# A causal mask moved from two bf16 products a row block into the VectorE row maximum

## The reference

```
phi    = tp @ W_combine.T                      # 512 x 64 features of a sequence
logits = einsum('bnd,bmd->bnm', phi, phi) * T / temp
logits = where(n >= m, logits, -inf)           # causal
attn   = softmax(logits)
out    = (attn @ V) @ W_out.T + b_out
```

## Time and profile before

| | before |
|---|---|
| median of 3 runs | 726.18 us (725.48 to 726.43) |
| span of the profiled execution, first to last instruction | 729.0 us |
| PE busy | 707.8 us (97%) |
| PE weight load busy | 558.7 us (77%) |
| DVE busy | 620.3 us (85%) |
| ACT busy, POOL busy | 424.9 us (58%), 387.0 us (53%) |
| mean granted TensorE clock | 0.992 of full speed |

### The profile page before, as it was taken

How to read it: one execution, slowest core, us unless ns; L and a number is a source line. 1 busy time by engine, 2 the same in 40 slices (tenths; PEclk the granted TensorE clock), 3 DMA queues, 4 the chain that set the end, 5 groups by cost and what they waited for, 6 DMA issues and landing times.

```text
span 729.0 us, 15002 instructions
## 1 busy us (share of the span) xinstructions
PE 707.8 (97%) x4592; PEld 558.7 (77%) x4592; DVE 620.3 (85%) x1899; ACT 424.9 (58%) x840; POOL 387.0 (53%) x828
## 2 busy tenths in 40 slices
PE   7998999999999999999999999999999999999896
PEld 4977777777797887778697787879788777867684
DVE  5887888788989898998989899898989899887865
ACT  4539475736456584656648574655757565565441
POOL 4526577363565646476564747556574646653300
PEclk9889999999999999999999999999999999999999
DMA  7341111112423050323214042322304132121004
GB/s 217 112 145 43 45 28 32 29 31 65 111 89 87 6 155 16 116 59 117 58 47 129 3 125 51 116 58 79 98 1 144 31 117 59 59 59 59 1 7 167
DMA packets 49110, 54.12 MB, mean 74 GB/s; under 512 B 6214, under 2 KB 40584, under 8 KB 49032
## 3 DMA queue, kind: packets, MB, share of 16 engines
q1 hardware_dynamic: 48258, 52.64, 25.7%
q10 hardware_dynamic: 774, 0.53, 0.3%
HBM read 20.65 MB, written 16.78 MB: 51 GB/s over the span
## 4 chain that ended last, share of the span: by engine, by line
PE 85%; DVE 5%; DMA 2%; ACT 2%; POOL 2%; issue 2%; SPq 0%; DVEq 0%; ACTq 0%; POOLq 0%
PE ps L438 17%; PE ps L317 16%; PE ps L343 15%; PE ps L466 6%; PE ps L409 6%; PE ps L515 5%; PE ps L500 4%; PE ps L579 4%; PE ps L388 4%; PE ps L559 2%; PE ps L478 2%; POOL Z L254 2%; PE ps L390 2%; DMA xmT<-Z 1%; DMA X<-in_x 1%
## 5 line engine op out<-in xcount | busy, mean ns | idle before, releaser
L438 PE MATMUL ps<-VS,ET 128*128 128x257 f32 x640 | 159.4, 383 | 0.8 <-ACT ET L769 0.5
L438 PEld LDWEIGHTS ps<-VS,ET 128*128 128x128 f32 x640 | 112.5, 189 | 24.3 <-issue 11.7
L254 POOL TENSOR_TENSOR Z<-Z,QB 128x512 f32<-128x512 f32 x60 | 76.5, 1275 | 98.0 <-ACT Z L750 96.3
L708 ACT ACTIVATE xn<-X,rs 128x256 f32<-128x256 f32 x128 | 66.3, 592 | 73.3 <-POOL rs L1322 73.2
L769 ACT ACTIVATE ET<-ps 128x128 f32<-128x128 f32 (+3 forms) x128 | 55.2, 436 | 69.3 <-PE ps L317 67.9
L343 PE MATMUL ps<-W1h,xh 128*128 128x354 f32 x256 | 88.9, 347 | 0.2 <-DVE xl L889 0.2
L902 DVE TENSOR_TENSOR VS<-ps,biasM 128x354 f32<-128x354 f32 x128 | 66.3, 522 | 24.8 <-PE ps L343 24.7
L759 ACT ACTIVATE E<-ps,nmax 128x128 f32<-128x128 f32 (+3 forms) x128 | 64.3, 525 | 35.7 <-DVE nmax L971 34.2
L343 PE MATMUL ps<-W1l,xh 128*128 128x354 f32 x256 | 84.2, 329 | 0.0
L343 PE MATMUL ps<-W1h,xl 128*128 128x354 f32 x256 | 83.3, 325 | 0.0
L264 POOL TENSOR_SCALAR xm<-X,rs 128x256 f32<-128x256 f32 x120 | 65.8, 562 | 4.7 <-POOL rs L1343 4.7
(11 more groups left out here) (210 smaller groups left out, 1678.9 us busy)
## 6 DMA issues: line engine op xcount, KB each, us to landing
X<-in_x SPq DMA_DIRECT2D x32, 512.0 KB, 4.3
xmT<-Z SPq DMA_DIRECT2D x120, 128.0 KB, 2.3
out_x<-X SPq DMA_DIRECT2D x30, 512.0 KB, 3.9
out_x<-X SPq DMA_DIRECT2D x4, 256.0 KB, 2.2
X<-in_gru_whhT SPq DMA_DIRECT2D x1, 768.0 KB
wih<-in_gru_wihT SPq DMA_DIRECT2D x1, 768.0 KB
X<-in_W_v ACTq DMA_DIRECT2D x1, 256.0 KB, 4.3
X<-in_W_outT ACTq DMA_DIRECT2D x1, 256.0 KB, 5.0
```

The costliest lines, as they stand in the source:

```text
L254: e.tensor_tensor(Z[:, i + 1, :], Z[:, i, :], QB[:, :], ALU.mult).then_inc(s["zm"], 1)
L438: ins = e.matmul(p[:, 0:D + 1], ET[:, r % 2, j * 128:j * 128 + 128], VS[:, (2 * k + d) % 4, j, 0:D + 1], start=j == 0, stop=j == i)
L708: ins = e.activation(xn[:, d, t, :], X[:, b % NX, t, :], ACT.Identity, bias=rs[:, d, 2, t:t + 1], scale=rs[:, d, 1, t:t + 1])
```

## The change

The two mask products of each row block and their constants `identb` and `maskb` go. In their place stands one SBUF tensor `causal` of 128 x 512 fp32: zero, and +1e30 above the diagonal in its last 128 columns. `U` gets the opposite sign, so that the logits in PSUM are negated. `row_max` is now an operation that adds the last w columns of `causal` to the w negated logits, writes the sum back over them in PSUM, and keeps the minimum of each row; this minimum is the `nmax` of before. `expo` reads with scale -1. The program lists of all engines are written out in other words (loop bounds as numbers, breaks elsewhere), and `warm` now holds the wait that stood ahead of it.

```diff
-        identb = sb("identb", [128, 3, 128], BF)
-        maskb = sb("maskb", [128, 3, 128], BF)
+        causal = sb("causal", [128, N])
...
                     for d in range(2):
                         at["lg", 8 * k + 2 * i + d] = banks[d][:, c:c + w]
                         e.matmul(banks[d][:, c:c + w], QK[own(d), 0, rows], QK[own(d), 1, 0:w], start=True,
-                                 stop=False, skip_group_check=True)
-                    for d in range(2):
-                        e.matmul(banks[d][:, c + w - 128:c + w], identb[own(d), 1 - d, :], maskb[own(d), 1 - d, :], start=False,
-                                 stop=False, skip_group_check=True)
-                    for d in range(2):
-                        e.matmul(banks[d][:, c + w - 128:c + w], identb[own(d), 2 - d, :], maskb[own(d), 2 - d, :], start=False,
                                  stop=True, skip_group_check=True).then_inc(s["lg_mm"], 1)
...
-                e.activation(E[:, r % 3, 0:w], at["lg", r], ACT.Exp,
-                             bias=nmax[:, r % 8:r % 8 + 1]).then_inc(s["E"], 1)
+                e.activation(E[:, r % 3, 0:w], at["lg", r], ACT.Exp, bias=nmax[:, r % 8:r % 8 + 1],
+                             scale=-1.0).then_inc(s["E"], 1)
...
-                e.tensor_reduce(nmax[:, r % 8:r % 8 + 1], at["lg", r], AX.X, ALU.max,
-                                negate=True).then_inc(s["nmax"], 1)
+                w = (n // 2 + 1) * 128
+                e.tensor_tensor_reduce(at["lg", r], at["lg", r], causal[:, N - w:N], 1.0, 3e38, ALU.add, ALU.min,
+                                       nmax[:, r % 8:r % 8 + 1]).then_inc(s["nmax"], 1)
...
-                e.tensor_scalar(U[:, :], U[:, :], tmp8[:, 8:9], None, ALU.mult).then_inc(s["soft"], 1)
+                e.tensor_scalar(U[:, :], U[:, :], tmp8[:, 8:9], -1.0, ALU.mult, ALU.mult).then_inc(s["soft"], 1)
...
-            e.affine_select(out=maskb[:, :, :], in_=maskb[:, :, :], compare_op=ALU.is_ge, fill=-1e30,
-                            base=-64, pattern=[[64, 3], [-1, 128]], channel_multiplier=1).then_inc(s["const_chain"], 1)
+            e.affine_select(out=causal[:, N - 128:N], in_=causal[:, N - 128:N], compare_op=ALU.is_ge, fill=1e30,
+                            base=0, pattern=[[-1, 128]], channel_multiplier=1).then_inc(s["const_chain"], 1)
```

More of the change, by code:

```diff
@@ L651, in _ @@
[L651 to L659, removed]
-                p, n, f, m, g = it + 2, it + 1, it, it - 1, it - 2
[L661 to L681, removed]
+            first_warm(); weights_setup(); xn_t(0, 0, 0); xn_t(0, 0, 1); bias_setup(); xn_t(0, 1, 0)
@@ L1256, in _ @@
-            attended(1, 3); phase(2); row_max(1, 7); turns(2); unwind(2); clamp(2); attended(1, 4)
-            lm_stats(1, 1); lm_stats(1, 2); xn_low(3, 1, 0); lm_stats(1, 3); top(0, 0, 0); top(0, 0, 1)
-            lm_stats(1, 4); attended(1, 5); lm_stats(1, 5); top(0, 1, 0); attended(1, 6); top(0, 1, 1)
-            lm_stats(1, 6); vs(3, 0, 0); attended(1, 7); weight_sum(0, 0); shift(0, 0); chosen(0, 0)
-            xn_low(3, 1, 1); vs(3, 0, 1); vs(3, 0, 2); shift(0, 1); qk_full(2); vs(3, 0, 3); xn_low(4, 0, 0)
@@ L1277, in _ @@
-            top(2, 0, 1); shift(2, 0); gates(1); top(2, 1, 0); candidate(1); top(2, 1, 1); attended(3, 4)
-            shift(2, 1); new_slots(1); lm_stats(3, 2); attended(3, 5); chosen(2, 0); weight_sum(2, 0)
-            for it in range(3, NP - 1):
+            xn_low(0, 0, 1); bias_setup(); xn_low(0, 1, 0); ln_stats(1, 1, 0); vs(0, 0, 0); ln_stats(1, 1, 1)
+            vs(0, 0, 1); vs(0, 0, 2); xn_low(0, 1, 1); vs(0, 0, 3); square_a_setup(); norm_sum(0, 0)
+            xn_low(1, 0, 0); vs(0, 1, 0); xn_low(1, 0, 1); vs(0, 1, 1); attention_setup(); vs(0, 1, 2)
@@ new lines, in _ @@
+            xn_low(3, 0, 1); row_max(1, 6); lm_stats(1, 0); xm_low(0, 1, 0); xm_low(0, 1, 1); attended(1, 3)
+            phase(2); row_max(1, 7); turns(2); unwind(2); clamp(2); attended(1, 4); lm_stats(1, 1)
+            lm_stats(1, 2); xn_low(3, 1, 0); lm_stats(1, 3); top(0, 0, 0); top(0, 0, 1); lm_stats(1, 4)
+            attended(1, 5); lm_stats(1, 5); top(0, 1, 0); attended(1, 6); top(0, 1, 1); lm_stats(1, 6)
+            vs(3, 0, 0); attended(1, 7); weight_sum(0, 0); shift(0, 0); chosen(0, 0); xn_low(3, 1, 1)
@@ new lines, in _ @@
+            vs(3, 0, 1); vs(3, 0, 2); shift(0, 1); qk_full(2); vs(3, 0, 3); xn_low(4, 0, 0); lm_stats(1, 7)
+            xm_low(1, 0, 0); row_max(2, 0); row_max(2, 1); row_max(2, 2); vs(3, 1, 0); vs(3, 1, 1)
+            row_max(2, 3); vs(3, 1, 2); vs(3, 1, 3); chosen(0, 1); attended(2, 0); xm_low(1, 0, 1)
+            lm_stats(2, 0); norm_sum(3, 0); weight_sum(0, 1); xm_low(1, 1, 0); row_max(2, 4); row_max(2, 5)
+            attended(2, 1); norm_sum(3, 1); xm_low(1, 1, 1); phase(3); turns(3); gathered(0); unwind(3)
@@ new lines, in _ @@
+            clamp(3); attended(2, 2); attended(2, 3); row_max(2, 6); lm_stats(2, 1); xn_low(4, 0, 1); gates(0)
+            row_max(2, 7); attended(2, 4); lm_stats(2, 2); lm_stats(2, 3); xn_low(4, 1, 0); candidate(0)
+            attended(2, 5); lm_stats(2, 4); top(1, 0, 0); lm_stats(2, 5); attended(2, 6); vs(4, 0, 0)
+            top(1, 0, 1); shift(1, 0); lm_stats(2, 6); xn_low(4, 1, 1); vs(4, 0, 1); new_slots(0); qk_full(3)
+            top(1, 1, 0); attended(2, 7); top(1, 1, 1); weight_sum(1, 0); slot_values(0); lm_stats(2, 7)
@@ L1280, in _ @@
+            finish(0, 1, 0); finish(0, 1, 1); lm_stats(3, 0); gathered(1); row_max(3, 6); lm_stats(3, 1)
+            row_max(3, 7); top(2, 0, 0); top(2, 0, 1); shift(2, 0); gates(1); top(2, 1, 0); candidate(1)
+            top(2, 1, 1); attended(3, 4); shift(2, 1); new_slots(1); lm_stats(3, 2); attended(3, 5)
+            chosen(2, 0); weight_sum(2, 0)
+            for it in range(3, 15):
                 p, n, f, m, g = it + 2, it + 1, it, it - 1, it - 2
@@ new lines, in _ @@
+                finish(g, 0, 1); row_max(n, 3); gates(m); vs(p, 0, 0); vs(p, 0, 1); vs(p, 0, 2); vs(p, 0, 3)
+                xn_low(p, 1, 0); candidate(m); attended(n, 0); xn_low(p, 1, 1); xm_low(f, 0, 0)
+                xm_low(f, 0, 1); finish(g, 1, 0); finish(g, 1, 1); vs(p, 1, 0); norm_sum(p, 0); row_max(n, 4)
+                vs(p, 1, 1); vs(p, 1, 2); vs(p, 1, 3); lm_stats(n, 0); norm_sum(p, 1); xm_low(f, 1, 0)
+                xm_low(f, 1, 1); row_max(n, 5); attended(n, 1); phase(p); turns(p); unwind(p); clamp(p)
```

266 lines of the change are left out of this document (129 added, 137 removed).

## The result

| | before | after |
|---|---|---|
| median | 726.18 us (725.48 to 726.57, 5 runs) | 722.4 us (721.55 to 724.04, 5 runs) |
| ratio after / before | | 0.9949, 95% interval 0.9932 to 0.9966 |
| span of the profiled execution | 729.0 us | 719.9 us |
| a round of the loop | 41.77 us | 41.63 us |

The change makes the kernel 0.5% faster. I had forecast 726.5, no change. The time lies in the range (721.5 to 735) and on the side to which I gave 0.20.

A forecast was written before the change was run, and what follows sets the result against it. PE was taken to bound the kernel, with DVE beside it almost without margin. Terms of +0.205, -0.065 and -0.12 gave +0.02 us a round, +0.3 over 16 rounds: forecast 726.5 us, range 721.5 to 735.

The forecast's parts named there:

- the rival of the halved rate: Row maximum reading and writing one PSUM bank streams at half rate: some 2 us a round, 758 us; chance 0.08.
- The second instruction: One-column second half of each new row maximum on DVE: extra time between 0.06 and 0.19 us, taken as 0.075.
- d: Extra DVE time of one new row maximum over the old: between 0.06 and 0.19 us, taken as 0.075.
- the rival at 722.2: DVE not on the path after all, or d only 0.03: a round gains 0.25 us; faster case, chance 0.20.
- stretch B: End of `phi` to next round's `proj(p,0,0)`: DVE, with margin 0.29 at `xn_low`, decides; -0.065 us a round.
- A: End of `proj(p,1,3)` to `values(n,6)`: three row maxima, margin 0.02, DVE decides; 3d - 0.02 = +0.205 us a round.
- rest: Block 2's mask products, with no row maximum ahead of a PE wait: -0.12 us a round, all to PE.
- (1): Sign in the profile: no mask products, and block 1's product right behind block 0's.
- (2): Sign on DVE: 128 more instructions, at most 128 d more busy time, the 512 wide pass about 690 ns.
- (3): Sign on DVE: from one row maximum to the next start 0.66 us for 512 columns, not 0.59.
- (4): Sign on PE: `values(n,6)` waits for `attended(n,4)` by some 0.4 us, `proj(p,0,0)` for `xn_low` by 0.15.
- (5): Sign in the loop: rounds of 41.8 us, with PE no longer busy throughout.

The follow-up runs named there:

- e4: The kernel before, unchanged, run and profiled again: 726.61 us, ratio 1.0002, a round of 41.76 us.
- e3: The changed kernel, unchanged, run and profiled again: 722.74 us, ratio 0.9948 to the kernel before, a round of 41.64 us.
- e1: The kernel before without its mask products, old row maximum kept, nothing masked: 721.49 us, ratio 0.9926, a round of 41.58 us.
- e9: The changed kernel with row maximum number 5 alone made a plain minimum without mask: 723.40 us, ratio 0.9959 to the kernel before.
- e10: The changed kernel with `row_max(n,5)` moved ahead of `vs(p,1,3)` on DVE: 723.86 us, ratio 0.9960 to the kernel before.
- e7: The changed kernel with `sine(p)` ahead of `probs_t(n,4)` on ACT and `lm_stats(n,2)` moved to the next round: 723.10 us, ratio 0.9943 to the kernel before.
- e11: The kernel of e10 with `lm_stats(n,2)` also moved to the next round: 719.79 us, ratio 0.9908 to the kernel before.
- e5: The changed kernel with `attended(f,7)` ahead of `ln_stats(p,1,1)` on DVE: 719.90 us, ratio 0.9906 to the kernel before.
- e13: The kernel before, mask products kept, with the DVE moves of e11 and e5: 724.86 us, ratio 0.9988 to the kernel before.

## Why the prediction was wrong

**Right:** that the full 9.0 us would not come; that PE, shown as busy throughout, had DVE beside it with almost nothing between; that block 2's part comes through; that `values(n,6)` follows `attended(n,4)` without a margin; that the pass streams at the old rate and that the PSUM write back costs next to nothing, so that the rival of the halved rate (758) is out.

**The step that failed** is "The second instruction": "between 0.06 and 0.19 ... A gain is excluded". I put the lower end by the `MATCH_VALUE_LOAD` pair, where the second half starts 0.06 after the first. The accumulator read starts at the very time of the next instruction, and d is 0.00 to about 0.03. With the measured d my own sum gives -0.28 a round (table below), 16 of them 4.5 us, and about 721.7; the rival at 722.2 (its d: 0.03) would have been near the forecast. That it came so close, 722.2 against 722.4, is partly luck. By its sum each round gains 0.25. The loop's gain 0.12 to 0.14, since **a second step failed, the margin of stretch B** (0.29 at `xn_low`), and the hand-placed rounds gain more than the sum gives them.

**The sum, term by term,** by the distances in e4 and e3:

| | predicted | same formula with measured d | measured |
|---|---|---|---|
| A, `logits` j = 2 to the next `phi` | +0.205 | 0.02 + 0.07 - 0.02 = +0.07 | +0.08 (12.85 to 12.93) |
| B, `phi` to `proj` | -0.065 | -0.23, all that PE gains there | -0.02 (9.47 to 9.45) |
| rest | -0.12 | -0.12 | -0.16 (19.43 to 19.27) |
| round | +0.02 | -0.28 | -0.12 (41.76 to 41.64), by the stretches -0.10 |

- *A*: that DVE decides was right, and e1 to e4 put the fused maxima at 0.06 a round. But of the three maxima of my sum only numbers 6 and 7 count on DVE's way (e9, e10), and the sum came out by small terms that cancel. That ACT's way through `expo(n,5)` was as tight beside it, I had not seen (e7, e10, e11). The 0.21 that PE was to gain here is 0.11.
- *B*: the formula measured the margin of the wrong pair. `xn_low` to `proj` had 0.29, but between `phi` and `proj` PE passes `out_mm`, whose bank `attended(f,7)` frees with 0.03 to spare (0.07 less the 0.04 of a semaphore). No row maximum stands ahead of it, so d does not count, and the gain is gone whatever the reduction costs (e1). Behind it GIN binds next (e5).
- *Rest*: block 2's step from the products to `proj(p,1,0)` gained 0.17 (9.03 to 8.86), not the 0.12 between the starts of two matmuls.
- *Rounds by hand*: I counted them like the loop's. They gained 0.34, 0.59 and 0.53, together as much as the eleven of the loop (1.4), and the two are most of the 4.4 us between the two profiles.

**What would show it**: (1) and (2) held, with 2.0 us more on DVE; (3) failed (0.60 and 0.65 for 0.66); (4) failed in both places, and the wait stood at a third; (5) failed, and "PE no longer busy throughout" was no test, since the waits hardly show in its busy time. The warning from *VectorE: DVE Perf Modes* of the Trainium skill against more operations, which I had set against the exchange, was worth 0.02 us an exchange here (2.0 us of DVE for 128); its section on two Vector instructions with no wait between them does say that an operation with an accumulator output is two instructions, and the trace agrees (256 for 128).

What stays open: how much of the 1.1 us ahead of the hand-placed rounds is the change's. That `phi` comes at 71.9 to 76.3 us in the four profiles with mask products and at 70.9 to 74.4 in the twelve without, so two profiles can't tell.

## What to carry to other kernels

When work leaves the busiest engine, ask at each of the next steps of that engine what its buffer or input waits for, and not only at the steps that the new work delays: here one such step swallowed the gain of stretch B with no new cost at all. Where two ways lead into a stretch, relieve both in one experiment before you call either harmless: singly each gave 0.00 to 0.01, together 0.32. And a change that moves little may be worth much more after the order around it is set anew: 0.12 a round became 0.49.

## What the hardware showed that I had not expected

- The read-out of an accumulated minimum (`DVE_READ_ACCUMULATOR2_ANT`, 141 ns long, one column) starts together with the next DVE instruction and does not delay its start (358.81 and 358.81, 385.51 and 385.51). Where the next one is a 512 wide pass of the same kind, that pass took 0.65 to its successor in place of 0.60; an `X` addition of 512 columns behind a read (358.81) took 0.60, as one without (361.44) did.
- The minimum reaches a waiting engine later than that of the plain reduction, though. The read of 377.97 ends at 378.11 and ACT, which waits for it, starts at 378.14, 0.65 after the pass. By the medians of the loop's rounds it is 0.65 in the changed kernel and 0.58 in the kernel before and in e9, both with the plain reduction.
- An add of PSUM and SBUF that writes back to the same PSUM columns ran at the rate of the reduction that only reads: 0.60 against 0.59 for 512 columns, 0.20 against 0.20 for 128. The 125 ns of overhead on PSUM that the Trainium skill gives (*Perfetto Trace Analysis*, optimizing Scalar/DVE operations) do not show here: from start to start it is 1.04 ns a column between 128 and 512 columns, which leaves 0.07.
- PE's busy time hides its waits. In e13 PE is busy for 41.59 of 41.59 us and in the kernel before for 41.77 of 41.77, with the same products in both.
